# Gated delta-rule visits: key and query products as one full-width product per head, query part seeded into the output banks by ScalarE, inversion and output norm on GpSimd

## The reference

```python
attn = -(einsum(k_beta, k) * decay_mask), lower part; attn = inverse of (1 - attn)
value_corrected = attn @ v_beta
k_cumdecay      = attn @ (k_beta * exp(g))
def chunk_step(state, c):
    qk = einsum('bhid,bhjd->bhij', q_c, k_c)
    intra = where(mask_upper1, 0.0, qk * dm_c)
    v_prime = v_c - einsum('bhld,bhde->bhle', kcd_c, state)
    inter = einsum('bhld,bhde->bhle', q_c, state) * ge_c[..., None]
    out = inter + einsum('bhij,bhjd->bhid', intra, v_prime)
    new_state = state * gel_c + einsum('bhld,bhle->bhde', k_c * kd_c, v_prime)
core = rmsnorm(core * silu(z)) ; out = core @ W_out
```

## Time and profile before

| | us |
|---|---|
| median of 3 runs (4161.04 to 4176.44) | 4169.28 |
| the profiled execution's own time | 4157.96 |
| its span | 4156.2 |
| TensorE busy | 3794.4 (91%) |
| VectorE busy | 2563.9 (62%) |
| ScalarE busy | 2176.8 (52%) |
| GpSimd busy | 943.5 (23%) |

### The profile page before, as it was taken

The page is one execution under the profiler, slowest core; times in us unless marked ns, Lnnn a source line. Parts: engine busy times, 40 slices in busy tenths (PEclk is TensorE's granted clock), DMA queues, the critical chain, the costliest instruction groups (busy, mean ns, idle before and its releaser), DMA issues. The chain is left out here.

```text
span 4156.2 us, 73250 instructions
## 1 busy us (share of the span) xinstructions
PE 3794.4 (91%) x25346; PEld 2785.3 (67%) x25346; DVE 2563.9 (62%) x6909; ACT 2176.8 (52%) x5705; POOL 943.5 (23%) x849
## 2 busy tenths in 40 slices
PE   7989988888985999979999999999999999979778
PEld 4555555555553666658888888888888888855344
DVE  4752468887335899856666666666666666532632
ACT  3741267776114666646666666665666666622222
POOL 0010000000001435342333323233233233221211
PEclk9999999999996999989999999999999999979879
DMA  2010100000004666543333333333333333222002
GB/s 80 2 35 0 50 1 2 2 2 16 20 1 129 211 219 207 219 137 92 97 74 92 80 90 91 82 94 97 81 95 83 86 90 81 61 86 80 20 29 92
DMA packets 443148, 322.82 MB, mean 78 GB/s; under 512 B 330208, under 2 KB 380064, under 8 KB 440736
## 3 DMA queue, kind: packets, MB, share of 16 engines
q1 hardware_dynamic: 439712, 309.75, 26.0%
q0 software_dynamic: 3072, 8.39, 0.6%
HBM read 200.13 MB, written 117.88 MB: 77 GB/s over the span
## 5 line engine op out<-in xcount | busy, mean ns | idle before, releaser
L2453 ACT ACTIVATE d_heads_VP<-d_heads_chain,d_GALL 128x128 f32<-128x128 f32 x512 | 189.0, 369 | 632.6 <-PE d_heads_chain L2347 629.2
L2596 DVE SCALAR_TENSOR_TENSOR d_heads_S<-d_heads_S,d_GALL,d_heads_chain 128x128 f32<-128x128 f32 x768 | 232.7, 344 | 381.3 <-PE d_heads_chain L2354 379.3
L2532 POOL TENSOR_TENSOR d_heads_KD<-d_heads_KR,d_GALL 128x512 f32<-128x512 f32 x256 | 270.0, 1075 | 284.2 <-ACT d_heads_KR L2421 284.2
L637 ACT ACTIVATE b_heads_PR<-b_heads_sc,b_heads_NM 128x128 f32<-128x128 f32 (+3 forms) x512 | 269.3, 534 | 114.8 <-DVE b_heads_NM L701 114.5
L2233 PE MATMUL d_heads_value<-all_XT,d_heads_WVZ 128*128 128x256 f32 x1024 | 292.6, 389 | 19.2 <-POOL d_heads_ZS L2511 19.2
L2378 PE MATMUL d_heads_projected<-d_heads_WO,d_heads_OT 128*128 128x256 f32 x1024 | 288.4, 395 | 20.2 <-ACT d_heads_OT L2472 20.2
L2020 DVE SCALAR_TENSOR_TENSOR d_front_CY<-d_front_proj,d_CW,d_front_CY 128x511 f32<-128x511 f32 (+2 forms) x384 | 271.9, 744 | 49.9 <-ACT d_front_CY L1931 45.4
L2574 DVE SCALAR_TENSOR_TENSOR d_heads_CY<-d_heads_value,d_CW,d_heads_CY 128x511 f32<-128x511 f32 (+2 forms) x384 | 283.1, 741 | 22.1 <-ACT d_heads_CY L2414 22.0
L2255 PE MATMUL d_heads_value<-d_heads_WVZ,all_XT 128*128 128x256 f32 x1024 | 284.6, 380 | 1.3 <-DVE d_heads_CY L2574 1.3
L2354 PEld LDWEIGHTS d_heads_chain<-d_heads_VP,d_heads_KD 128*128 128x128 f32 x1792 | 262.9, 191 | 31.0 <-ACT d_heads_VP L2453 9.5
L2354 PE MATMUL d_heads_chain<-d_heads_VP,d_heads_KD 128*128 128x128 f32 x1792 | 277.2, 277 | 5.9 <-ACT d_heads_VP L2453 5.9
(11 more groups left out here) (348 smaller groups left out, 8908.6 us busy)
## 6 DMA issues: line engine op xcount, KB each, us to landing
...
d_heads_GE<-d_gerows SPq DMA_DIRECT2D x128, 256.0 KB, 5.3
...
d_heads_ITB<-d_it SPq DMA_DIRECT2D x128, 128.0 KB, 2.8
...
```

The source lines that it names most:

```text
L637: nc.scalar.activation(PR[p % 3][j][:, at:at + w], SC[p % 2][j][:, at:at + w], ACT.Exp, bias=NM[:, u % 2, t, slot:slot + 1], scale=-1.0 if ...
L2532: nc.gpsimd.tensor_tensor(KD[i % 2][:, 4 * q:4 * q + 4, h, :], KR[q][:, :, :], decay, ALU.mult).then_inc(kds, 1)
L2596: stt(S[:, h, :], S[:, h, :], gate(i, GEL0 + h, c), R[h][:, HD:2 * HD], ALU.mult, ALU.add).then_inc(su, 1)
```

## The change

In `d_heads`:

1. Keys and queries of a chunk lie side by side in `KQ` (now `[P, NCH, 4, CHUNK]`: queries, keys, keys, queries), so for each head one product with 128 weight columns gives the keys' part in its own half of the partitions and the queries' part in the other half, in the bank `R[h]`. The two 64-column pairs (L2333, L2336) go. For head 1 the order is reversed, so output rows and `ITB`, `SZ`, `WO` swap halves.
2. The query part is multiplied by exp(g) (`GEX`, a ninth kind in `GALL`) and written to the output bank by ScalarE, one copy per head and chunk (`seeded`), and the output product adds to it (`start=False`). For chunk 0 VectorE clears the place (`blank`). `QS`, `GE` and the table `gerows` go.
3. `UU` is made per head, on 64 partitions each; the increments and key products raise one semaphore per head. The U product goes to a third part of `R[0]` and waits for both `UU` and the first seed, the output product for the second.
4. The inversion steps go from VectorE to GpSimd, in the same slots. `YN` goes from ScalarE (eight copies a visit) to GpSimd (two multiplies by a broadcast), behind `RM`.

In `d_front`: the squared lengths are made with a 32-column weight of ones against the squares (four groups of 32 output rows), copied to SBUF by ScalarE (`RW`) and turned by two products with columns of the identity; this runs one visit behind. `norms` of a key head goes from its last visit to the first of the next, and `scale` goes before `root`. In `d_gates` the transpose, copy and four stores of exp(g) go, and four copies into `GALL` come.

```diff
@@ d_gates
-            act.wait_ge(turned, 2)
-            nc.scalar.copy(rowse[:, :, :], ebank[:, :].rearrange("p (q n) -> p q n", q=TB)).then_inc(rows, 1)
             for c2, h in pairs:
                 nc.scalar.copy(place(GALL, KDEC0 + h, c2, h), of(kd, c2, h)).then_inc(placed, 1)
+                nc.scalar.copy(place(GALL, GEX, c2, 1 - h), of(ge, c2, h)).then_inc(placed, 1)
@@ d_front, TensorE
+            def square_rows(i):
...
+                for q in range(4):
+                    mm = nc.tensor.matmul(SSQ[q * HB:(q + 1) * HB, 0:2 * P], ones[:, :],
+                                          SQ[i % 2][:, 2 * q:2 * q + 2, :, :].rearrange("p c k n -> p (c k n)"),
+                                          start=True, stop=True)
+                mm.then_inc(srow, 1)
             def lengths(i):
-                for c in range(NCH):
-                    at = (g % 2) * 32 + b * NCH + c
-                    mm = nc.tensor.matmul(SSQ[:, at:at + 1], SQ[i % 2][:, c, :, :].rearrange("p k n -> p (k n)"),
-                                          ones[:, :], start=True, stop=True)
+                pe.wait_ge(rowc, i + 1)
+                for m in range(2):
+                    at = 2 * P + (g % 2) * 32 + b * NCH + m
+                    mm = nc.tensor.matmul(SSQ[:, at:at + NCH - 1:2], RW[i % 2][:, m, :], C.ident[:, 0:P:HB],
+                                          start=True, stop=True)
@@ d_front, VectorE
-                if b == 3:
-                    norms(g)
+                if b == 0 and g >= 1:
+                    norms(g - 1)
@@ d_heads, SyncE
-                sp.dma_start(KQ[i % 3][:, :, :, :].rearrange("p c k n -> p (c k n)"), kq_d[i]).then_inc(kql[i % 3], 16)
-                for h in range(GROUPS):
-                    sp.dma_start(GE[i % 2][:, h, :], head_rows(gerows, g, h, P)[:, b * SEQ:(b + 1) * SEQ]
-                                 ).then_inc(gel[i % 2], 16)
+                src = kq_d[i].rearrange("p (c k n) -> p c k n", c=NCH, k=3)
+                sp.dma_start(KQ[i % 3][:, :, 1:4, :], src).then_inc(kql[i % 3], 16)
+                sp.dma_start(KQ[i % 3][:, :, 0, :], src[:, :, 2, :]).then_inc(kql[i % 3], 16)
@@ d_heads, TensorE
+            for x in OI:
+                nc.tensor.matmul(x[:, :], C.ident[:, :], XT[:, 0, 0:SEQ], start=True, stop=True).then_inc(first, 1)
...
-                            mm = nc.tensor.matmul(R[0][hrows(h), 0:HD], kq[:, c, 0, :], S[:, h, :], start=True, stop=True)
-                        mm.then_inc(kss, 1)
-                        for h in range(GROUPS):
-                            nc.tensor.matmul(inter[hrows(h), :], QS[i % 2][:, c, h, :], S[:, h, :], start=True, stop=False,
-                                             skip_group_check=True)
+                        nc.tensor.matmul(R[h][:, 0:HD], kq[:, c, 2 - 2 * h:4 - 2 * h, :].rearrange("p k n -> p (k n)"), S[:, h, :],
+                                         start=True, stop=True).then_inc(kss, 1)
...
-                        pe.wait_ge(uu, 7 * i + c)
+                        pe.wait_ge(seeded, 14 * i + 2 * (c - 1) + 1)
+                        pe.wait_ge(uu, 14 * i + 2 * c)
@@ d_heads, ScalarE
+                if sub == 0 and c > 0:
+                    if c == 4 and i > 0:
+                        act.wait_ge(yo, 2 * i)
+                    for h in range(GROUPS):
+                        other = hrows(1 - h)
+                        act.wait_ge(kss, 14 * i + 2 * (c - 1) + h + 1)
+                        nc.scalar.activation(OI[c // 4][other, (c % 4) * HD:(c % 4 + 1) * HD], R[h][other, 0:HD], ACT.Copy,
+                                             scale=GALL[other, i // BATCH, i % BATCH, GEX, c:c + 1]).then_inc(seeded, 1)
@@ d_heads, GpSimd
+                nc.gpsimd.tensor_tensor(YN[:, :, :], YO[q % 2][:, :, :], RM[:, :].unsqueeze(2).broadcast_to([P, 4, HD]), ALU.mult
+                                        ).then_inc(yn, 1)
...
+                            inverse(g + 1, k)
@@ d_heads, VectorE
-                    dve.wait_ge(kss, 7 * i + c)
-                    stt(UU[:, :], R[0][:, 0:HD], gate(i, NGE, c), VB[i % 2][:, c, :], ALU.mult, ALU.add).then_inc(uu, 1)
+                    for h in range(GROUPS):
+                        own = hrows(h)
+                        dve.wait_ge(kss, 14 * i + 2 * (c - 1) + h + 1)
+                        stt(UU[own, :], R[h][own, 0:HD], GALL[own, i // BATCH, i % BATCH, NGE, c:c + 1], VB[i % 2][own, c, :],
+                            ALU.mult, ALU.add).then_inc(uu, 1)
```

200 lines of the change are left out of this document (99 added, 101 removed).

## The result

The changed kernel takes 4244.52 us (median of four runs, 4239.82 to 4247.01), the kernel before 4165.16 us in the same measurement (4160.75 to 4176.44). The ratio is 1.0185, with a 95% interval of 1.0164 to 1.0205. The predicted median was 4173 us. The time lies above the forecast's own range (4150 to 4198) and just above the whole one (4100 to 4240), and the kernel is slower.

What follows compares the result with a forecast made beforehand. Two of eight chunks were held set by ScalarE, the others by TensorE's order and the chain. Visits +8, first matmuls +2, front -4 and -4, gates +2 gave 4162 us profiled, 4173 median; own range 4150 to 4198, whole 4100 to 4240.

Steps and rivals of the forecast that it cites:

- From the key product to the U product: Part of each recurrence chunk: 1.10 us for 1.13, TensorE's saving of 0.25 us lost to the second UU update.
- Seeds: ScalarE's 14 copies a visit, 0.27 us each: free where ScalarE idles, a cost in chunks 5 and 7.
- A pair costs 0.54: Two seed copies without idle cover on ScalarE: 0.54 us more, making chunk 5 4.16 us and chunk 7 4.28.
- A visit: One gated visit of eight chunks: 28.85 us for 28.73, so 64 x 0.12 = +8 us.
- Inversion: 900 steps moved from VectorE to GpSimd: gains 0.6 us a visit; steps take 0.6 us and GpSimd keeps up.
- Rival B: GpSimd becomes the bound in the visits: at 1.0 us a step, 64 us more, 4237 us; chance 0.12.
- Output norm: YN copies moved from ScalarE to two GpSimd multiplies a visit: costs and gains nothing, being covered.
- Front: The front stage: -4 us over the key heads and -4 us at its end, where the power leaves the scaling's path.
- the visit with the exponential: Front visit set by ScalarE: shrinks by about 0.7 us, since its squares no longer wait for TensorE.
- Gates +2, first matmuls +2: Gates stage +2 us for four copies of 64x256; two full-bank matmuls at the visits' start +2 us.
- Rival A: ScalarE does not bind, seeds cost nothing in chunks 5 and 7: visit 27.7 us, total 4101 us; chance 0.26.
- Rival C: ScalarE and VectorE clash reading the same banks: 0.1 us more in each of seven chunks, 4218 us; chance 0.20.

Runs made afterwards that it cites:

- b_best: b_all with each head's state update started when its own increment is there, without waiting for both: 4073.25 us, ratio 0.9779 to the kernel before.
- a_swap: The changed kernel with the U product's two waits in the other order, first both UU updates, then the seed: 4232.14 us, ratio 1.0157.
- a_noseed: The changed kernel without ScalarE's seeds and the waits for them, so the output's query part is left out: 4142.47 us, ratio 0.9941.
- b_gpinv: The kernel before with only the gated visits' 900 inversion steps moved to GpSimd: 4127.83 us, ratio 0.9910.
- b_all: The kernel before with the new front and with inversion and output norm on GpSimd, recurrence unchanged: 4103.45 us, ratio 0.9851.
- b_f16: The kernel before with the new front's order, but the sums of squares kept as 16 passes: 4150.11 us, ratio 0.9956.

## Why the prediction was wrong, point by point

The kernels form a ladder, each rung measured. From the kernel before: front -22, inversion -34, norm none once the inversion has moved, separate state updates -30. All together, in b_best, they gave -94 (the kernel before varies by 5 us between the three measurements). That is 4073 us. From there to the change: the full-width product with two UU updates in place of one, without seeds and scaled queries, +11 (4073 to 4084, a net of what the product saves and the second update costs, and the intervals of the two overlap), that the updates stand on different partitions +58 (to 4142), seeds +90 (to 4232), the waits' order +12 (to 4244). The kernels at 4084 and 4142 leave out a part of the work, as said above. **The recurrence's new form costs 171 us and hides the 94 us that the rest earns.**

- *From the key product to the U product, "UU of head 1 starts at 0.69 ... the U product starts at 1.10".* This step failed, in every chunk. Measured is 1.37 to 1.38, and 1.30 in the last two steps. UU of head 0 starts at 0.50 for 0.43 (0.42 in the last two steps): in chunks 2 and 3 behind the convolution, which the prediction had counted there; in the others VectorE idles ahead of it, and why it starts late is not shown. The pair takes 0.72 us for 0.61, since I took the spacing of the state updates, which stand on the same partitions. The product starts 0.15 us after the pair for 0.06, with two waits where I counted one signal. Together 0.27 us (0.18 behind a convolution), and with the parts around it the chunks 0 to 4 take 14.60 us for 13.59: 1.0 of the 1.47 us that a visit is over the prediction. The other two thirds of the chunk came out as said (1.10 and 1.16 for 1.14).
- *The row that could have told.* The prediction shows "64x128 in 0.53 us for two" and does not ask whether the two overlap. One ZS copy lasts 0.26 us, as its line shows, so two in 0.53 stand end to end. They are on different partitions, as the two UU updates are. It is ScalarE's row and not VectorE's, so it was a hint and no proof:

```profile
L2431 ACT COPY d_heads_ZS<-d_heads_turned x128: 245/260/263, 1823.7 to 3629.2; 64x128 f32<-64x128 f32 x128
```

- *Seeds: "Where ScalarE idles they cost nothing".* Right but for the order of the two waits: 3.57 us in chunks 0 to 1, 1 to 2 and 3 to 4 in a_swap and in a_noseed. *"A pair costs 0.54"* was too little: a pair takes 0.69, since a seed lasts 0.33 us where a ZS copy lasts 0.26. Chunk 4 to 5 came out at 4.18 for 4.16, and that is luck: the pair cost 0.71 us there, and the rest shrank to 3.47 us for 3.62, by 0.12 because `SZ` had changed its halves (see the last section). 6 to 7 came out at 4.40 for 4.28, 5 to 6 at 3.42 for 3.18, 7 to 0 at 3.50 for 3.50. In the third visit the turned copy adds 0.85 us and not 0.6.
- *A visit* is 30.32 us on average for 28.85: 64 x 1.47 = 94 us over the prediction's +8.
- *Inversion: 0.6 us a visit gained, steps of 0.6 us on GpSimd.* Right: in b_gpinv the mean visit falls from 28.70 to 28.10 us, and the steps take 0.48 and 0.51. Rival B never came near, and GpSimd waited 581 us for the norm's sums alone between 1900 and 3600 us.
- *Output norm: "nothing".* Right where the inversion has moved too (b_all); wrong by 18 us where it has not.
- *Front, -4 for the heads and -4 for its end.* The heads gave -20.6 and the end -1.6. The term that was mis-sized is the visit with the exponential, "shrinks by about 0.7": without inversion it takes 9.28 us for 11.14, 1.9 less (order alone, in b_f16, gives 10.40). The norms do lengthen the next head's visit, by 0.6 without inversion (6.98 for 6.35) and by up to 1.5 with it. The first head, which I had not costed, gave 8 us in this execution. The end's -4 failed too: the power no longer stands ahead of the scaling, but it stands behind it, and the stage still waits for both.
- *Gates +2, first matmuls +2:* +2, and -1 from the front's end to the first V' copy.
- *Rival A* had ScalarE bound nowhere: it is bound in the two steps named, and it holds the third visit's turned copy. *Rival C* had the right place (the chain between the key product and the U product) and the right sign, and a size a third of the true one (0.1 us a chunk for 0.27); its mechanism is refuted by a_noseed.

On the sum, +94 (visits), -17 (front's heads), +2 (its end) and -3 (first matmuls) come to +76 us over the predicted 4162 us of the profiled execution; with the 8 of the end stage it is 4246, and that execution took 4247.
